# An attention stage whose steps are ordered anew: each engine reads only what TensorE made a step earlier

## The reference, cut to what matters

```python
h = _layer_norm(x, g1, b1)
q = (h @ Wq + bq).reshape(n, NH, HD)
k = (h @ Wk + bk).reshape(n, NH, HD)
v = (h @ Wv + bv).reshape(n, NH, HD)
e = jnp.sum(q[d_all] * k[s_all], axis=-1) / np.sqrt(HD)     # s_all, d_all: the edges, and a loop at each node
...
x = residual + att
h = _layer_norm(x, g2, b2)
ffn = gelu(h @ W1 + bf1, approximate=False) @ W2 + bf2
```

## The kernel before, in words

| part | engine | lag before |
|---|---|---|
| statistics, aggregation | DVE | 3 |
| `std` | ACT | 3 |
| `rstd`, `shift` | DVE | 4 |
| normalize, both | ACT | 4 |
| turn rows | PE | 5 |
| `srcT`; `carry` | ACT; DVE | 5 |
| `p_q`, `p_ks`, `p_kd` | PE | 6 |
| `qT`; `prod` | ACT; DVE | 6 |
| `p_sum` | PE | 7 |
| `logits` | ACT | 8 |

## Time and profile before

### The profile page before, as it was taken

How to read it: one execution, slowest core, us unless ns; L and a number is a source line. 1 busy time by engine, 2 the same in 40 slices (tenths; PEclk the granted TensorE clock), 3 DMA queues, 4 the chain that set the end, 5 groups by cost and what they waited for, 6 DMA issues and landing times. The chain is left out here.

```text
span 2872.0 us, 49421 instructions
## 1 busy us (share of the span) xinstructions
PE 2193.6 (76%) x14363; PEld 1777.0 (62%) x14363; DVE 1930.2 (67%) x7755; ACT 1328.2 (46%) x3166; POOL 1228.6 (43%) x1416
## 2 busy tenths in 40 slices
PE   2478777548887677728888806878849999999998
PEld 2355555348887566715656606777737777777776
DVE  3589999736665577736666694444547777777775
ACT  0489999712222244436656600000015656656655
POOL 3544434146652666445455103555543333333332
PEclk9789999879998899958888857888969999999999
DMA  3478888668775466624333104445432333333331
GB/s 92 133 213 244 243 239 250 178 184 232 232 229 175 125 197 199 185 94 119 110 119 117 58 9 116 131 145 153 130 123 83 106 111 104 106 111 102 108 111 49
DMA packets 354022, 413.95 MB, mean 144 GB/s; under 512 B 51578, under 2 KB 235278, under 8 KB 353754
## 3 DMA queue, kind: packets, MB, share of 16 engines
q1 hardware_dynamic: 316186, 340.50, 37.9%
q0 software_dynamic: 34496, 69.37, 9.1%
q10 hardware_dynamic: 3072, 0.92, 0.1%
HBM read 264.11 MB, written 179.90 MB: 155 GB/s over the span
## 5 line engine op out<-in xcount | busy, mean ns | idle before, releaser
L1746 PEld LDWEIGHTS p_y<-w,g_T 128*128 128x128 f32 x3136 | 365.4, 192 | 46.4 <-issue 24.2
L1746 PE MATMUL p_y<-w,g_T 128*128 128x128 f32 x3136 | 365.8, 275 | 0.0
L1764 ACT ACTIVATE nT<-p_n 128x512 f32<-128x512 f32 x98 | 58.5, 597 | 644.8 <-PE p_n L1754 644.8
L1739 PE MATMUL p_f<-nT,w 128*128 128x512 f32 x784 | 354.4, 595 | 0.0
L548 POOL DMA_INDIRECT x_dst<-in_x_dram,idx x196 | 189.0, 964 | 283.0 <-DMA edge_x<-x_dst 200.4
L1729 POOL TENSOR_TENSOR rstd<-var,minus_half 128x4 f32<-128x4 f32 x98 | 113.4, 1157 | 450.1 <-ACT res L1777 450.0
L1771 ACT ACTIVATE g_T<-p_f,bf 128x512 f32<-128x512 f32 x392 | 267.1, 681 | 31.5 <-PE p_f L1739 31.4
L1131 POOL DMA_INDIRECT x_src<-x_rows,idx x196 | 185.1, 944 | 210.5 <-ACT normed L1219 113.9
L1550 POOL DMA_INDIRECT x_rows<-xv,idx x196 | 197.3, 1007 | 160.5 <-DVE xv L1636 104.4
L902 POOL DMA_INDIRECT h_src<-h_table,idx x196 | 192.4, 982 | 156.2 <-POOLq L123 57.2
L894 POOL DMA_INDIRECT e_h<-in_x_dram,idx x172 | 168.3, 979 | 178.8 <-DVE msg L1010 78.4
(11 more groups left out here) (309 smaller groups left out, 5874.0 us busy)
## 6 DMA issues: line engine op xcount, KB each, us to landing
xs<-x_rows SPq DMA_DIRECT2D x98, 512.0 KB, 3.6
x_in<-in_x_dram SPq DMA_DIRECT2D x98, 256.0 KB
h_table<-h_rows SPq DMA_DIRECT2D x98, 256.0 KB
x_rows<-x_in SPq DMA_DIRECT2D x98, 256.0 KB, 2.9
out_dram<-res SPq DMA_DIRECT2D x98, 256.0 KB, 2.1
x_rows<-x_rows SPq DMA_DIRECT2D x50, 500.0 KB
edge_x<-x_dst SPq DMA_DIRECT2D x98, 128.0 KB
h_own<-edge_x SPq DMA_DIRECT2D x49, 256.0 KB
```

Source lines behind the costliest of these rows:

```text
L1739: e.matmul(p_f[ch][:], w_1[:, ch * P:(ch + 1) * P], nT[:, g % 2, :], start=True, stop=True).then_inc(f_prod, 1)
L1746: mm = e.matmul(p_y[g % 2][:, a * D:(a + 1) * D], g_T[:, g % 2, ch, a * P:(a + 1) * P], w_2[:, ch, :], start=(ch == 0), stop=(ch == FCH - 1))
```

## The change

Lags and orders are new, and some buffers are more:

| part | engine | lag after | place in the engine's step |
|---|---|---|---|
| statistics, aggregation | DVE | 3 | destination first, source and aggregation last |
| `std` | ACT | 4 | fourth |
| `rstd`, `shift` | DVE | 5 (NORM) | between the `carry` calls and behind them |
| normalize | ACT | 6 | destination third, source fifth |
| turn rows | PE | 7 (TURN) | second, destination before source |
| `srcT`; `carry` | ACT; DVE | 8 (CARRY) | second; in turn with `prod` |
| `p_q`, `p_ks`, `p_kd` | PE | 9 (PROD) | third |
| `qT`; `prod` | ACT; DVE | 10 | first; in turn with `carry` |
| `p_sum` | PE | 11 (SUM) | first |
| `logits` | ACT | 12 | last |

STEPS becomes GE + 13. [...] `x_src` and `x_dst` have seven buffers, `rows` eight, `mv` four. SP loads `x_dst` ahead of `rows`. No instruction that computes is added or removed. The core of the diff:

```diff
-            SN, ON = 6, 4
+            SN, RN, ON = 7, 8, 4
...
+                p_src = [ps(f"p_src{s}", c) for s in range(2)]
+                p_dst = [ps(f"p_dst{s}", c) for s in range(2)]
+                p_q, p_kd, p_ks, p_sum = (ps(name, c) for name in ("p_q", "p_kd", "p_ks", "p_sum"))
...
                 AHEAD = 3
-                OUT = AHEAD + 3
-                STEPS = GE + AHEAD + 6
+                NORM = AHEAD + 2
+                TURN = NORM + 2
+                CARRY = TURN + 1
+                PROD = CARRY + 1
+                SUM = PROD + 2
+                STEPS = GE + SUM + 2
...
                 @block.tensor
                 def _(e):
                     for n in range(STEPS):
+                        if at_step(n, SUM):
+                            k = n - SUM
+                            e.wait_ge(prod_s_ready, k + 1)
+                            e.wait_ge(prod_d_ready, k + 1)
+                            wait(e, logit_ready, k)
+                            for j in range(GT):
+                                for a in range(2):
+                                    at = (j * 2 + a) * HEADS
+                                    mm = e.matmul(p_sum[:, at:at + HEADS], prod[:, k % 2, a, j * P:(j + 1) * P], head_sum[:],
+                                                  start=True, stop=True)
+                            mm.then_inc(summed, 1)
+                        if at_step(n, TURN):
+                            k = n - TURN
+                            e.wait_ge(dst_normed, k + 1)
+                            wait(e, dstT_ready, GT * (k - 1))
...
                             e.wait_ge(src_normed, k + 1)
-                            wait(e, srcT_ready, k)
+                            wait(e, srcT_ready, k - 1)
...
-                        if at_step(n, AHEAD + 3):
-                            k = n - AHEAD - 3
+                        if at_step(n, PROD):
+                            k = n - PROD
                             e.wait_ge(dstT_ready, GT * (k + 1))
                             wait(e, qT_ready, k)
...
                 @block.scalar
                 def _(e):
                     for n in range(STEPS):
+                        if at_step(n, PROD + 1):
+                            k = n - PROD - 1
+                            e.wait_ge(q_prod, k + 1)
...
+                        if at_step(n, CARRY):
+                            k = n - CARRY
                             e.wait_ge(src_turned, k + 1)
...
+                        if at_step(n, NORM + 1):
+                            k = n - NORM - 1
                             e.wait_ge(shift_ready, k + 1)
...
+                        if at_step(n, SUM + 1):
+                            k = n - SUM - 1
+                            e.wait_ge(summed, k + 1)
+                            e.activation(logits[:, group(k) * GT:(group(k) + 1) * GT, :].rearrange("p j h -> p (j h)"),
+                                         p_sum[:, 0:GT * 2 * HEADS], ACT.Copy).then_inc(logit_ready, 1)
```

More of the change, by code:

```diff
@@ L1087, in attention @@
                 prod = sb("prod", [P, 2, 2, GROUP], F32, c)
-                p_dst, p_src, p_q, p_kd, p_ks, p_sum = (ps(name, c) for name in ("p_dst", "p_src", "p_q", "p_kd", "p_ks", "p_sum"))
-                rows_in = sems("rows_in", SN, c)
+                p_src = [ps(f"p_src{s}", c) for s in range(2)]
+                p_dst = [ps(f"p_dst{s}", c) for s in range(2)]
+                p_q, p_kd, p_ks, p_sum = (ps(name, c) for name in ("p_q", "p_kd", "p_ks", "p_sum"))
+                rows_in = sems("rows_in", RN, c)
                 dst_in = sems("dst_in", SN, c)
@@ L1124, in _ @@
                 def _(e):
[L1125 to L1133, removed]
+                    for k in range(GE):
+                        wait(e, src_normed, k - SN + 1)
+                        for j in range(GT):
+                            t = group(k) * GT + j
+                            e.indirect_dma_start(out=x_src[:, k % SN, j, :], out_offset=None, in_=x_rows,
+                                                 in_offset=bass.IndirectOffsetOnAxis(ap=idx[:, X_SRC, t:t + 1], axis=0))\
+                                .then_inc(gathered[k % SN], 16)
                 @block.sync
@@ L1148, in _ @@
                                 .then_inc(dst_in[k % SN], 16)
+                            wait(e, dstT_ready, GT * (k - RN + 1))
+                            e.dma_start(rows[:, k % RN, :, :], edge_row(group(k), TO_NEXT, TO_NEXT + 1)).then_inc(rows_in[k % RN], 16)
                     for k in range(ON):
@@ L1176, in _ @@
                             e.matmul(p_kd[:], w_vqk[:, 2 * D:3 * D], dstT[:, k % ON, :], start=True, stop=True).then_inc(kd_prod, 1)
[L1177 to L1187, removed]
                 @block.scalar
@@ L1285, in _ @@
[L1285 to L1300 removed]
+                            k = n - AHEAD
@@ L1302, in softmax @@
+                            e.wait_ge(stats_ready, 2 * (k + 1))
+                            wait(e, shift_ready, k - 3)
+                            for j in range(2 * GT):
+                                ins = e.bn_aggr(mv[:, k % 4, j, :], stats[:, k % 2, j, :])
+                            ins.then_inc(mv_ready, 1)
         def softmax(logits, alpha):
```

132 lines of the change are left out of this document (56 added, 76 removed).

## The result

| | before | after |
|---|---|---|
| time of one execution, median of 4 | 2486.8 us (2485.97 to 2490.35) | 2703.8 us (2700.17 to 2704.66) |
| ratio, 95% interval | | 1.088 (1.086 to 1.089) |
| span of the profiled execution | 2872.0 us | 2702.6 us |
| stage `attention` in it | 397.2 us | 512.3 us |

A forecast was written before the change was run, and what follows sets the result against it. Before, clean attention steps of 5.41 us ended last in a ScalarE-VectorE ring, with TensorE at 5.19. A new ring with clock loss, 43 x (11.2 - 5.41) = 249, plus 15 for fill and drain, gave +264: 2751 us, range 2609 to 2795.

The forecast's parts named there:

- The ring: Attention: `p_sum`, transposes, `p_q`, then ACT's whole step to `logits` must fit one step; 8.48 us instead of 5.41, 43 steps.
- The clock term: Attention: PE's pause of about 3 us each step lowers its clock, adding 2.7 us; period 11.2, ends 10.6 and 11.9.
- the ring case: Attention: ring with drops of the clock, 2751 us, own range 2695 to 2786; chance 0.65 with drops.
- Fill and drain: Attention's start and end: four more steps cost +15 us, with 10 and 20 as ends.
- The view of timed runs: Attention before: profiled stalls are mostly absent when timed; 295 us instead of 397.2, pace 5.41 us, up to 6.0.
- The rest of the change: Attention's second banks, lags and buffers: mostly slack, gaining at most 0.22 us a step down to TensorE's 5.19.
- no ring: Rival: an order or count was misread, so attention's TensorE runs at 5.19 us a step; 2493 us, chance 0.04.
- VectorE sets the pace: Rival: with no ring, attention's steps take VectorE's 4.87 us; 2479 us, chance 0.02.

The follow-up runs named there:

- e1: The changed kernel with `logits` moved from last to first place of ACT's step: 2485.7 us, ratio to before 1.0003.
- e2: The changed kernel with `p_sum` moved from first to last place of PE's step, `logits` still last on ACT: 2487.6 us, ratio 1.0006.
- e3a: The changed kernel with one bank for `p_src` instead of two: 2704.0 us, ratio 1.087.
- e3: The changed kernel with one bank for `p_src` and three useless products behind `p_kd` in each step: 2662.6 us, ratio 1.072.
- e0: The kernel before, unchanged, profiled once more: one execution, 2484.9 us, span 2483.2 us.
- e7: The changed kernel with one bank for `p_src` and four useless products behind `p_kd` in each step: 2649.6 us, ratio 1.067.

## Why the prediction was right, and where its sizes were off

**The ring** is as the prediction laid it out: its engines, its order, both waits, 43 turns (the 44th `p_sum` starts at 1529.36, and the next steps are 6.9, 5.2 and 4.4 us). e1 and e2 cut it at one end each, and the loss is zero both times; e3a shows that the second bank of `p_src` has no part in it. Of its terms ACT's step was 4.54 us instead of 4.66: in rows 3 it starts anew after gaps, and without gaps an instruction starts some 0.1 us before the one ahead of it has ended (`qT` 1238.24 for 0.69, `srcT` 1238.83). At full clock the ring was put at 8.48 us and is 8.43 (e3).

**The clock term** was the mis-sized step. The prediction took 2.7 us a step and 11.2 in all. No run shows the 2.7: measured are 10.30, so 1.9 on top of 8.43. The 43 steps make 39 of the 47 us by which the forecast was too high, 37 of them by the clock and 2 by the ring. The direction was right (in the 43 steps each half-clock stretch does fall on the head of the ring: the 42 of them begin between 1.3 us before a start of `p_sum` and 2.8 us behind it), but the length was taken from the stretches at five gaps of before, 6.8 us or more, as the one of rows 11 at 0.50; there `p_sum` takes 3.45 us instead of 1.85. The stage had eight gaps of 2.7 us or more, not the five of rows 10, and it had shorter stretches too, behind shorter gaps. A gap of 1.80 us in the timeline of before, and the window behind it:

```profile
1324.89 0.66 PE L1160 MATMUL p_src<-ident,normed 128*128 128x128 f32 x4 [1.80 <-ACT normed L1219]
1325.55:1328.97 3.42, 3.42 (x8) 1.86 (x7) 3.01 (x21) 2.80 (x7) 2.50 (x4) 0.50 0.43 123
```

In the kernel after it is the same mixture: of the 42 stretches 12 are 6.8 us, as the one from 1231 on, and 29 are half of that, 3.4 us (the first is 10.2): in the turn of 1242.93 only `p_src`, `p_q` and what stands beside them are slow. The head of the ring is then only partly covered. The turn from 1231.31 is one that was covered whole: 6.93 us instead of 3.63, so 3.3 more, where the upper end of the prediction, 11.9 us, has 3.4. Nor is the pause the same with either clock, as the prediction has it: it is 3.0 us where the keys ran at full clock and 2.0 to 2.2 where they ran partly at half (2.20 before 1231.31), and the clock fell behind both.

**Some luck** is in the time. A period of 10.30 us lies under the whole of the clock term's own range, 10.6 to 11.9: with 5.41 before, its lower end gives 43 x 5.19 + 10 = 233 us, 2720. The 2703.8 measured lies in the range of the ring case, from 2695 on, only because that allowed for a timed pace of 6.0 before, and e0 shows 5.40. The range as a whole, from 2609 on, did allow for less clock than that.

**Fill and drain**: +15 forecast, with 10 as the lower end; +9.9 and -0.9 measured. That is 6 of the 47 us. Why the fill grew by less was not looked into.

**The view of timed runs** held: 295 us for the stage by clean steps, 290.8 in e0. Without that step, 397.2 us would have been the base, and the change would have looked like 115 us.

**The rest of the change** was put at a gain of at most 0.22 us a step on PE's own pace. e1 shows 0.21 less in the clean steps. Of the rivals, "no ring" was 2493 us by that sum; without the ring it is 2486, 7 less, of which 6 are again the fill and drain. "VectorE sets the pace" is answered too: in e1 PE is busy 99.5% of the time and its weight loads only 143.13 of 200 us, 72%, and the steps stayed at 5.19 us, the sum of PE's starts.

The row `p_sum L1167 <- logits L1229`, 44 times, is a gap of PE that comes back in every step, and the buffer behind it is the one bank of `p_sum`. That looks like one buffer too few. But e1 closed it with no bank more, by the place of the release, and e2 by that of the writer. No run gave `p_sum` a second bank, though e3a, at 2704.0 us with one bank less for `p_src`, shows that one could be spared for it; whether that would have cured the changed kernel as well is not shown.

Not shown: why the first profile of the kernel before was 385 us long. It did not come back in e0, nor in any other profile here; the spans of these lie within 8 us of their medians.

## What to carry to other kernels

In the timelines above an engine's lines come in the order of its block, as ACT's from L1201 to L1229 in the turn from 1238.24 to 1242.78. So for each single buffer between two engines, write down where its writer and its reader stand in their steps, and follow the queues from one to the other and back. Here a return wait that is one step old was free where the way from the writer, over the first thing that the other engine waits for, through that engine's queue to the release was shorter than a step, and cost the difference where it was longer (8.43 us at full clock against PE's own 5.19, e3 and e1); a reader placed last and a writer placed first put nearly both steps into it, 3.6 of PE's 5.2 us and all of ACT's 4.5 here. Do this again for every buffer after each move: here rings came up through `p_sum`, through `p_dst` and through `p_kd`, and where one was cut, it was by an order or a bank at one end.

## What the runs showed of the hardware

In the changed kernel PE's clock fell beside pauses of 2.0 to 3.0 us (the first 4.6). It also fell in e3, in 18 of 43 steps of 8.2 to 10.1 us, where no pause was over 0.43 us (the clock of that middle is 0.92), while in e7, with the same work and one product more, 43 steps without a pause stayed at 1.00. A pause alone was not enough everywhere: in layer 2, pauses of 1.74 us left the clock at 1.00. Nor was the work of `p_sum` alone: e1 and e7 do it with hardly a pause, at 1.00. What tells layer 2 from this stage was not separated, as all their matmuls differ.

Filling a pause with useless matmuls made a kernel with a fixed ring faster, 2704.0 to 2649.6 us, though its PE then had no time left at all.
